# Key rotation sums on VectorE, a later root on GpSimd, the condition loaded by ScalarE: two conditioned attention layers on one core

## The reference

```python
# layer 0: 8 query heads and 1 key/value head of 64, MLP of 2048
h = ada_rms(x, time_emb, ln1_w, ln1_tw)
q = apply_rope(q, pos_ids)
k = apply_rope(k, pos_ids)
attn = jax.nn.softmax(scores, axis=-1)
x = res + ctx @ Wo.T
h = ada_rms(x, time_emb, ln2_w, ln2_tw)
x = res + jax.nn.silu(h @ Wg.T) * (h @ Wu.T) @ Wd.T
# layer 1: 16 query heads and 4 key/value heads of 32, latent keys and values, no MLP
h = (x - mu) * jax.lax.rsqrt(var + LN_EPS)
h = h * (1.0 + scale[:, None, :]) + shift[:, None, :]
c_kv = h @ Wkd.T
q = q * cos + _rotate_half(q) * sin
k = k * cos + _rotate_half(k) * sin
out = y.transpose(0, 2, 1, 3).reshape(B, T, C) @ Wo.T
return x + out
```

## Time and profile before

| | |
|---|---|
| runs shown | 902.44, 905.38, 907.66 us; median 905.38 |
| the profiled execution | 901.88 us, its span 900.1 us |
| instructions | 16086 |
| mean granted clock of TensorE | 0.998 of full speed |
| loaded and stored | 68.0 and 4.2 MB |

### The profile page before, as it was taken

The page is one execution under the profiler, slowest core; times in us unless marked ns, Lnnn a source line. Parts: engine busy times, 40 slices in busy tenths (PEclk is TensorE's granted clock), DMA queues, the critical chain, the costliest instruction groups (busy, mean ns, idle before and its releaser), DMA issues.

```text
span 900.1 us, 16086 instructions
## 1 busy us (share of the span) xinstructions
PE 878.1 (98%) x6190; PEld 736.7 (82%) x6190; DVE 569.8 (63%) x943; ACT 470.2 (52%) x862; POOL 414.8 (46%) x315
## 2 busy tenths in 40 slices
PE   8898999999999999999999999999999999998997
PEld 5787888888888888887887888888888888888885
DVE  5775556556556556567456676585774765757886
ACT  5666446455445445445537556455464464444662
POOL 3566545445435445446447545453444344431331
PEclk9999999999999999999999999999999999999999
DMA  9901222122222221122132222221222222100001
GB/s 343 333 24 40 103 81 82 71 82 83 71 83 83 71 82 72 71 71 88 71 117 71 71 71 83 71 83 52 68 83 71 83 83 71 69 3 13 25 25 36
DMA packets 31003, 73.19 MB, mean 81 GB/s; under 512 B 4304, under 2 KB 4816, under 8 KB 30928
## 3 DMA queue, kind: packets, MB, share of 16 engines
q1 hardware_dynamic: 30208, 72.07, 23.0%
q10 hardware_dynamic: 720, 0.09, 0.1%
HBM read 67.96 MB, written 4.19 MB: 80 GB/s over the span
## 4 chain that ended last, share of the span: by engine, by line
PE 83%; issue 6%; DVE 5%; POOL 4%; ACT 2%; DMA 0%; POOLq 0%; ACTq 0%; DVEq 0%
PE ps L484 25%; PE ps L486 24%; PE ps L485 24%; PE ps L763 2%; PE ps L590 1%; PE ps L572 1%; PE ps L741 1%; PE ps L751 1%; PE ps L557 1%; POOL qr L343 1%; PE ps L717 1%; POOL qr L395 1%; PE ps L690 1%; POOL stat L317 1%; POOL kr L394 1%
## 5 line engine op out<-in xcount | busy, mean ns | idle before, releaser
L360 POOL TENSOR_TENSOR gul<-rgu,guh 128x1024 fp32r<-128x1024 f32 x64 | 156.4, 2444 | 187.8 <-ACT guh L1453 187.8
L1067 DVE TENSOR_TENSOR xres<-ps,xres 128x512 f32<-128x512 f32 x256 | 174.6, 687 | 88.2 <-PE ps L486 88.2
L484 PE MATMUL ps<-h2h,guh 128*128 128x512 f32 x512 | 205.8, 402 | 0.7 <-issue 0.7
L486 PE MATMUL ps<-h2l,guh 128*128 128x512 f32 x512 | 199.7, 390 | 0.0
L485 PE MATMUL ps<-h2h,gul 128*128 128x512 f32 x512 | 199.5, 390 | 0.0
L486 PEld LDWEIGHTS ps<-h2l,guh 128*128 128x128 f32 x512 | 96.1, 188 | 20.8
L484 PEld LDWEIGHTS ps<-h2h,guh 128*128 128x128 f32 x512 | 96.2, 188 | 20.3 <-issue 1.1
L485 PEld LDWEIGHTS ps<-h2h,gul 128*128 128x128 f32 x512 | 96.3, 188 | 18.7
L484 PE MATMUL ps<-wdh,ah 128*128 128x512 f32 x256 | 101.0, 394 | 1.2 <-DVE al L1062 1.2
L1475 ACT CAST ah<-af 128x512 fp32r<-128x512 f32 x64 | 39.7, 621 | 119.2 <-DVE af L1080 119.2
L486 PE MATMUL ps<-wdl,ah 128*128 128x512 f32 x256 | 99.8, 390 | 0.0
(11 more groups left out here) (172 smaller groups left out, 1688.7 us busy)
## 6 DMA issues: line engine op xcount, KB each, us to landing
rgu<-gu SPq DMA_DIRECT2D x64, 512.0 KB, 3.6
rwd<-WdT SPq DMA_DIRECT2D x64, 256.0 KB, 2.7
xt<-xT SPq DMA_DIRECT2D x16, 256.0 KB, 3.1
out<-xres SPq DMA_DIRECT2D x15, 256.0 KB, 2.3
xres<-x SPq DMA_DIRECT2D x1, 2560.0 KB, 16.2
adaw<-adaT SPq DMA_DIRECT2D x1, 2048.0 KB, 10.3
wst<-WqkvT SPq DMA_DIRECT2D x4, 320.0 KB, 6.0
adaw<-ln_twT SPq DMA_DIRECT2D x4, 256.0 KB, 4.2
```

Source lines behind the costliest of these rows:

```text
L360: pool.tensor_tensor(gul[i][:, :], rgu[i][:, :], guh[i][:, :], ALU.subtract).then_inc(m_gul, 1)
L484: pe.matmul(dst, lh, rh, start=start, stop=False)
L486: return pe.matmul(dst, lh, rl, start=False, stop=stop)
L1067: dve.tensor_tensor(at, bank(BD[i % 2]), at, ALU.add).then_inc(m_x, 1)
```

## The change

VectorE adds the keys' part of the rotation itself, in both layers, right after the products, once it has waited for their end; new signals `a_kr` and `b_kr` tell TensorE. In layer 0 it writes the key twice from one broadcast read. GpSimd is left with the queries' 512 columns. In step 9 of layer 1 GpSimd's root of tile 12 goes behind the sum, and VectorE's `mean_rstd(12)` behind `add_out(8)`. ScalarE issues the load of the condition ahead of its other loads, and SyncE no longer issues it.

```diff
--- before.py
+++ after.py
@@ -160,6 +160,7 @@
          a_ssq2, a_ms2, a_rstd2, a_xn2, a_x2T, a_gf, a_h2h, a_h2l) = [sem("a_" + n) for n in (
             "ssq ms rstd cs hf hh hl qkv rope v qr qkT qT kT sc max ds ex sum rec p pTr pT ctx ch cl "
             "wo x ssq2 ms2 rstd2 xn2 x2T gf h2h h2l").split()]
+        a_kr, b_kr = sem("a_kr"), sem("b_kr")
 
         (m_guh, m_gul, m_wdh, m_wdl, m_gate, m_up, m_sg, m_af, m_ah, m_al, m_down, m_x) = [
             sem("m_" + n) for n in "guh gul wdh wdl gate up sg af ah al down x".split()]
@@ -256,7 +257,6 @@
                 cols = slice(D // 2 * h, D // 2 * (h + 1))
                 sp.dma_start(out[(NT - 1) * P:NT * P, cols], xres[:, NT - 1, cols]).then_inc(b_st, 16)
 
-            sp.dma_start(condt[:, :, :], by_row(condT)).then_inc(ld_cond, 16)
             for k in range(KT):
                 sp.dma_start(adaw0[:, k, :], by_row(ln1_twT)[:, k, :]).then_inc(ld_ln1[k], 16)
             load_xT(0)
@@ -339,9 +339,7 @@
                 pool.wait_ge(a_rope, t + 1)
                 wait(pool, a_qkT, t)
                 u, v = (tile[:, :, :, :].rearrange("p c h d -> p (c h d)") for tile in (t1, t2))
-                nk = D + HD0
-                pool.tensor_tensor(qr[:, 0:nk], u[:, 0:nk], v[:, 0:nk], ALU.add)
-                pool.tensor_tensor(qr[:, nk:nk + HD0], u[:, D:nk], v[:, D:nk], ALU.add).then_inc(a_qr, 1)
+                pool.tensor_tensor(qr[:, 0:D], u[:, 0:D], v[:, 0:D], ALU.add).then_inc(a_qr, 1)
 
             def low_wo():
                 pool.wait_ge(w0h, KT + 1)
@@ -391,7 +389,6 @@
                 pool.wait_ge(b_rope, t + 1)
                 wait(pool, b_qkT, t)
                 part = lambda tile, a, b: tile[:, :, a:b, :].rearrange("p c h d -> p c (h d)")
-                pool.tensor_tensor(kr1[:, :, :], part(u1, 8, 10), part(u2, 8, 10), ALU.add)
                 pool.tensor_tensor(qr1[:, :, :], part(u1, 0, 8), part(u2, 0, 8), ALU.add).then_inc(b_qks, 1)
 
             def clear_bdv1():
@@ -455,11 +452,9 @@
                 if u < TAIL:
                     rstd1(u + 2)
                 fill(pieces, f1 - min(f1, 2))
-                if u == TAIL:
-                    rstd1(u + 3)
                 if in_layer(u + 1):
                     rope_sum1(u + 1)
-                if u > TAIL and in_layer(u + 3):
+                if u >= TAIL and in_layer(u + 3):
                     rstd1(u + 3)
                 if u == TAIL:
                     fill(pieces, 2)
@@ -552,6 +547,7 @@
 
             def qk_T(t):
                 pe.wait_ge(a_qr, t + 1)
+                pe.wait_ge(a_kr, t + 1)
                 pe.wait_ge(a_v, t + 1)
                 for k in range(KT):
                     pe.transpose(ps[:, XB[0], P * k:P * (k + 1)], qr[:, P * k:P * (k + 1)], idn[:, :])
@@ -712,6 +708,7 @@
 
             def qk_T1(t):
                 pe.wait_ge(b_qks, t + 1)
+                pe.wait_ge(b_kr, t + 1)
                 pe.wait_ge(b_v, t + 1)
                 for g in range(4):
                     pe.transpose(ps[:, banks1(t)[0], P * g:P * (g + 1)],
@@ -1014,6 +1011,12 @@
                 dve.tensor_tensor(t2[:, :, :, half:HD0], q[:, :, :, 0:half], tab(1, half, HD0),
                                   ALU.mult).then_inc(a_rope, 1)
 
+                dve.wait_ge(a_rope, t + 1)
+                key = lambda tile: (tile[:, :, :, :].rearrange("p c h d -> p (c h d)")[:, D:D + HD0].unsqueeze(1)
+                                    .broadcast_to([P, 2, HD0]))
+                dve.tensor_tensor(qr[:, D:D + 2 * HD0].rearrange("p (i d) -> p i d", i=2), key(t1), key(t2),
+                                  ALU.add).then_inc(a_kr, 1)
+
             def keys(t):
                 dve.wait_ge(a_qkT, t + 1)
                 wait(dve, a_sc, t)
@@ -1131,6 +1134,9 @@
                 dve.tensor_tensor(u2[:, :, :, 0:half1], q[:, :, :, half1:HD1], tab1(1, 0, half1), ALU.mult)
                 dve.tensor_tensor(u2[:, :, :, half1:HD1], q[:, :, :, 0:half1], tab1(1, half1, HD1),
                                   ALU.mult).then_inc(b_rope, 1)
+                dve.wait_ge(b_rope, t + 1)
+                key = lambda tile: tile[:, :, 8:10, :].rearrange("p c h d -> p c (h d)")
+                dve.tensor_tensor(kr1[:, :, :], key(u1), key(u2), ALU.add).then_inc(b_kr, 1)
 
             def sc_view1(t):
                 at = banks1(t)[0]
@@ -1299,8 +1305,6 @@
                     softmax_scale1(u)
                 if u > TAIL and in_layer(u + 3):
                     stats1(u + 3)
-                if u == TAIL:
-                    mean_rstd(u + 3)
                 if u == -1:
                     add_x(NT - 1)
                 if in_layer(u - 1):
@@ -1338,6 +1342,7 @@
         @block.scalar
         def _(act):
 
+            act.dma_start(condt[:, :, :], condT.rearrange("(k p) n -> p k n", p=P)).then_inc(ld_cond, 16)
             act.dma_start(posi[:, :], pos).then_inc(ld_pos, 16)
             act.dma_start(invt[:, :], invf).then_inc(ld_pos, 16)
             act.dma_start(idn[:, :], ident).then_inc(ld_idn, 16)
```

## The result

The changed kernel takes 906.35 us (median of 20 executions), the kernel before 904.54 us (20 executions beside them): ratio 1.0024, 95% interval 1.0015 to 1.0034, so 2.2 us slower by the ratio (the two medians are 1.8 us apart). The forecast was 3.0 us faster. It is near rival 1, which had +2.4 us. The profiled execution took 904.93 us (span 903.1), 3.0 us more than the one of before.

What follows compares the result with a forecast made beforehand. TensorE is busy 98% of the span, so time changes only where it stands still or runs slow. Terms -3.0 - 1.0 - 0.6 - 0.9 + 0.3 + 1.2 + 1.0 = -3.0 us gave 902.4 us; range 899.0 to 909.0.

Steps and rivals of the forecast that it cites:

- rival 1: In layer 1's steps 10 to 14 GpSimd's queries' sum gets the port before the scaling: +6.4 us, total +2.4; chance 0.28.
- Step 9: Layer 1: GpSimd's sum no longer waits behind the root, TensorE's stop goes and the clock stays up: -3.0 us.
- Rival 4: The clock still falls in step 9 of layer 1: that step gives 2.3 us, total -2.3; chance 0.09.
- The head: Layer 0's first steps: earlier rotation sums gain 2.5 us in steps -1 to 3; step 5 loses 0.3.
- Step -1: Layer 0: the sum gets in ahead of VectorE's split of a weight, so the transposes start earlier: -0.9 us.
- step 4: Layer 0: gains nothing, because ScalarE's copies of gu set the queries' copy.
- Step 5: Layer 0: VectorE's work behind the rotation comes later and delays the first MLP matmul: +0.3 us.
- Rival 3: The head gives nothing, as transfers or ScalarE bind: 2.5 us of steps -1 to 3 gone, total -0.5; chance 0.09.
- The condition's load: Start of the kernel: ScalarE issues it first, so invf lands later and the chain of the head starts later: +1.2 us.
- Rival 2: The condition's load costs its slot alone, 0.45 us, and everything else holds: total -3.75 us; chance 0.14.
- Layer 1's steps -1 to 8: VectorE's added 0.32 us is hidden by a gap while it waits for TensorE: no change.
- Steps 10 to 14: Layer 1's end: VectorE is packed, the key sum delays the scaling by 0.32 us in steps 10 to 12: +1.0 us.

Runs made afterwards that it cites:

- The last experiment but one: Kernel before with root behind the sum and layer 0's keys on VectorE, plus the condition's load issued by ScalarE third: ratio 0.9953 to the kernel before.
- The half-sum run: Changed kernel with GpSimd's 512-column queries' sum made as twice 256 from tile 11 on: ratio 0.9999 to the kernel before, 2.3 us less than the changed kernel.
- the two good parts: Kernel before with only step 9's root behind the sum and layer 0's key sum on VectorE; run twice: ratios 0.9926, then 0.9956 to the kernel before.
- the best version: Kernel before with step 9's root behind the sum and layer 0's key sum on VectorE for tiles 0 to 5 only: ratio 0.9934, 898.03 us.
- the root alone: Kernel before with only step 9's root (and VectorE's mean_rstd) moved behind the rotation sum: ratio 0.9967 to the kernel before, 3.0 us less.

## Why the prediction was wrong

**Step 9, -3.0 us: right,** in size and by its steps (15.35 to 12.35, the sum at 818.41, the clock at 1.00), alone and in every combination. Rival 4 didn't happen: the 0.43 us that TensorE still stands before the scores (0.6 predicted) is followed by no fall in any profile with the root behind the sum.

**The head, -2.5 + 0.3: nearly right,** -1.88 measured. Step -1 gave 0.88 (0.9 predicted), step 0 0.55 (0.6), steps 1 to 3 0.29, 0.31 and 0.21 (0.34 each). Missed: step 4. "Step 4 gains nothing" was read as neutral, but ScalarE's copies there fix the scores' start, so 0.4 of what had been gained before is given back (the transposes had gained 2.4 by then, the scores of step 4 only 2.0). Step 5 lost the predicted 0.3. Rival 3 is refuted.

**The condition's load, +1.2: right,** 1.15 by the means, 1.44 in the pair of profiled executions. The landings scatter by 1.4 us within one order of issue, so that the single pair came so near is in part luck. Rival 2's slot alone (0.45) is refuted by the later issue of 0.6 us and the longer landing behind it; the Trainium skill, DMA: Bandwidth & Descriptors, "Issuing engines are not separate DMA queues", gives only the sequencer's time as what another issuer saves. The last experiment but one fits its other half, that all queues end on the same engines: the same 64 KB landed in 2.0 to 2.6 us ahead of the weights and in 5.72, in one execution, behind their start.

**Layer 1's steps -1 to 8, nothing: right,** +0.03. Layer 0's steps from 6 on, too: from tile 7's rotation to layer 1's first pass 346.59 us before and 346.43 after.

**Steps 10 to 14, +1.0: this is the step that failed,** by 5.4 us. Its words were that "the scaling and all behind it come 0.32 us later" and that "the queries' sum can again start only when the scaling ends". The first is true of VectorE's queue and holds to 0.01 us when the order is enforced. The second is false: it held before only because the scaling was issued 0.16 us ahead of GpSimd's sum. The key sum makes the scaling's own request 0.32 us later, which puts it 0.16 us behind, and GpSimd's whole sum goes first, in all five steps: 1.43, 1.42, 1.43, 1.08 and 1.05 us by the pieces, where rival 1 had 1.43 three times, 1.0 and 1.1. (Rival 1's start of the scaling, 847.05, does not fit its own 1.43; 846.98 does.) The prediction had both orders before it and gave the winning one 0.28, since the earlier trace rows showed VectorE coming in between GpSimd's operations. What the runs put in place of that: whichever operation asks first has the port for one instruction. The half-sum run shows both directions in one step. The Trainium skill, SBUF — State Buffer, "SBUF: two separate sides", states just this, and the traces now agree with its order as well as with the exclusion: 2.32, 1.76 and 1.22 us for the same scaling behind 512, 256 and no columns of GpSimd. A rule by which a waiting engine is served ahead of the next instruction of the engine that holds the port would give the same orders in these end steps; nothing here parts the two.

The net: +3.0 us between the profiled executions, +2.2 by the ratio.

## What to carry to other kernels

When two engines share a port, an added instruction costs no more than its own length only if it leaves the order at the port alone. Look for what the other engine asks for between the old and the new moment at which the next instruction asks, and add what that costs to the price: here 0.32 us of delay let in a wait of 1.10. Where such a loss is found, a wait that fixes the order, or splitting the other engine's instruction, shows it cheaply. And cut the span at an event that occurs in every step: compared between kernels, these pieces placed differences of 0.3 us that medians with 4 us of scatter could not.

## What the runs showed of the hardware

The same instructions with the same stops are granted different clocks from one execution to the next. TensorE's windows behind the last rotation, first of layer 1's keys back on GpSimd, then of the two good parts' second run, cut at the same distance from that rotation:

```profile
887.72:889.72 2.00, 0.66 (x4) 1.00 0.03 8
889.72:891.72 2.00, 1.94 (x20) 0.56 0.16 59
891.72:893.72 2.00, 1.32 (x18) 0.50 0.20 76
```

```profile
886.32:888.32 2.00, 0.66 (x4) 1.00 0.03 8
888.32:890.32 2.00, 1.27 (x20) 1.00 0.16 59
890.32:892.32 2.00, 1.99 (x27) 1.00 0.20 76
```

Both stand still for 1.34 us of the first window; in one the clock falls to 0.50 behind it, in the other it does not, and the end is 23.98 or 21.38 us long. Such a fall costs 2.6 us, as much as most of this case's effects: with one execution of each kernel, the best version could have looked no better than the root alone.
